# Second pass over an adjacency matrix: units of 8 rows with 2 KB runs in place of 16 rows with 1 KB runs

## The reference, cut to what matters

```
x = layernorm(x + (1 - 0.1 * x - 0.01 * sum(x * (adj @ x), axis=1)))        # layer 0, needs all of adj
x = layernorm(x + gnn(x, adj))                                              # layer 1, needs all of adj again
# in gnn, with A = adj without its diagonal:
node_support = concat(A_pos @ h, A_neg @ h)      # A_pos = (A > 0), A_neg = (A < 0), as 0/1
edge_output  = gru(node_support, h)
att          = softmax over each row of leaky_relu(... a) where A is not zero
edge_support = (att * A) @ (h @ W)
node_output  = gru(edge_support, h)
out          = diag(adj) * edge_output + diag(adj) * node_output
```

## Time and profile before

| | before |
|---|---|
| median of 3 runs | 1680.99 us |
| the profiled execution | 1673.49 us, span 1671.7 us |
| mean granted TensorE clock in it | 0.963 |
| TensorE busy | 1445.0 us (86%) |
| VectorE busy | 1368.0 us (82%) |
| ScalarE busy | 1163.8 us (70%) |
| moved by DMA | 550.18 MB, 329 GB/s over the span |

### The profile page before, as it was taken

One profiled execution on the slowest core, in us unless ns is written; L12 is line 12 of the kernel. 1 busy time (PEld: TensorE's weight loads), 2 busy tenths in 40 slices (PEclk: granted clock), 3 DMA queues, 4 the chain that ended last, 5 costly groups with the idle time before them and its releaser, 6 DMA issues.

```text
span 1671.7 us, 22680 instructions
## 1 busy us (share of the span) xinstructions
PE 1445.0 (86%) x6262; PEld 794.9 (48%) x6262; DVE 1368.0 (82%) x1335; ACT 1163.8 (70%) x1409; POOL 178.0 (11%) x226
## 2 busy tenths in 40 slices
PE   7987878887888888558998899899999899999995
PEld 6655656555555555224444444444444444444442
DVE  5999899898989898647878877887788788778874
ACT  6987979797979797436666666666566666666662
POOL 2000000000001010201101111110111011111100
PEclk9999999999999999779999999999999999999996
DMA  9999999999999999999999999999999999999980
GB/s 264 418 421 422 410 422 409 421 410 421 411 421 413 419 413 419 233 200 333 303 288 306 292 293 296 308 288 291 299 305 298 299 302 295 297 300 310 293 215 11
DMA packets 366090, 550.18 MB, mean 329 GB/s; under 512 B 71024, under 2 KB 333184, under 8 KB 333296
## 3 DMA queue, kind: packets, MB, share of 16 engines
q1 hardware_dynamic: 190672, 408.49, 70.5%
q10 hardware_dynamic: 174976, 141.05, 33.1%
q0 software_dynamic: 416, 0.36, 0.1%
HBM read 545.66 MB, written 4.19 MB: 329 GB/s over the span
## 4 chain that ended last, share of the span: by engine, by line
DMA 30%; issue 21%; ACTq 15%; DVE 15%; PE 9%; ACT 7%; SPq 2%; DVEq 1%; POOL 0%; POOLq 0%
DMA ring<-in_adj 18%; ACTq L247 12%; DMA h_rows<-final 11%; DVE at L806 7%; DVE ps L610 5%; ACT mask L932 5%; PE ps L572 5%; SPq L247 2%; PE ps L1033 2%; ACTq L950 1%; PE ps L539 1%; ACTq L946 1%; PE ps L1045 1%; ACTq L989 0%; ACT final L970 0%
## 5 line engine op out<-in xcount | busy, mean ns | idle before, releaser
L932 ACT ACTIVATE mask<-at 128x2048 fp32r<-128x2048 uint32 x256 | 489.4, 1913 | 281.2 <-DVE at L806 189.6
L572 PE MATMUL ps<-mask,parts 128*128 128x512 f32 x2048 | 552.0, 413 | 101.9 <-DVE ps L610 68.2
L610 DVE SCALAR_TENSOR_TENSOR ps<-ring,ps 128x2048 f32<-128x2048 f32 x256 | 584.3, 2301 | 55.3 <-PE ps L572 34.8
L806 DVE STREAM_TRANSPOSE at<-ring 128x2048 f32<-128x2048 f32 x256 | 577.8, 2290 | 43.6 <-POOL ring L719 37.9
L1033 PE MATMUL ps<-at,hk 128*64 128x512 f32 x2048 | 495.6, 620 | 79.7 <-DVE final L813 42.3
L506 ACT ACTIVATE at<-ring 128x2048 bf16<-128x2048 f32 x256 | 488.7, 1909 | 97.0 <-DMA ring<-in_adj 52.5
L572 PEld LDWEIGHTS ps<-mask,parts 128*128 128x128 f32 x2048 | 374.9, 193 | 278.8 <-DVE ps L610 203.8
L1033 PEld LDWEIGHTS ps<-at,hk 128*64 128x64 f32 x2048 | 148.7, 141 | 346.1 <-issue 250.8
L1045 PE MATMUL ps<-mask,parts 128*128 128x512 f32 x1024 | 270.2, 405 | 13.6 <-ACT final L959 12.9
L1045 PEld LDWEIGHTS ps<-mask,parts 128*128 128x128 f32 x1024 | 182.1, 188 | 152.1 <-issue 73.4
L719 POOL TENSOR_TENSOR ring<-ring,not_diag 128x256 f32<-128x256 f32 x128 | 93.8, 733 | 715.0 <-DMA ring<-in_adj 715.0
(11 more groups left out here) (152 smaller groups left out, 645.4 us busy)
## 6 DMA issues: line engine op xcount, KB each, us to landing
ring<-in_adj SPq DMA_DIRECT2D x256, 1024.0 KB, 16.2
ring<-in_adj SPq DMA_DIRECT2D x264, 512.0 KB, 10.7
ring<-in_adj ACTq DMA_DIRECT2D x248, 512.0 KB, 14.3
stage<-h_rows ACTq DMA_DIRECT2D x16, 128.0 KB, 16.3
nat<-h_rows ACTq DMA_DIRECT2D x16, 128.0 KB, 15.8
out<-final ACTq DMA_DIRECT2D x16, 128.0 KB, 15.4
h_rows<-final ACTq DMA_DIRECT2D x7, 256.0 KB, 22.7
hk<-h_rows ACTq DMA_DIRECT2D x7, 256.0 KB, 23.9
```

What stands on the lines that cost most here:

```text
L572: last = nc.tensor.matmul(ps[:, 4 * (n % 2) + i, :], pair[:, t % 2, e, :], x2[:, cols], start=e == 0, stop=e == 1)
L610: nc.vector.scalar_tensor_tensor(out=gram, in0=ring[:, i % RING, :], scalar=1.0, in1=gram, op0=ALU.mult, op1=ALU.mult, accum_out=flat[:, b ...
L806: nc.vector.transpose(b["at"][:, half % 4, :, :].rearrange("p c (f q) -> p f c q", q=Q), raw[:, :, HC * part:HC * part + HC, :]).then_inc( ...
L932: nc.scalar.activation(b["mask"][:, half % MS, :, :].rearrange("p c i -> p (c i)"), b["at"][:, half % 4, :, :].rearrange("p c i -> p (c i) ...
```

## The change

A unit is now 16 chunks of half the rows of a block: 8 rows for each partition, with runs of 512 columns, 2 KB. It is 2 MB as before, a block still has 8 units, and the ring holds four. Units 2w and 2w + 1 are the two halves of the rows of the same 16 chunks. A transposition takes 8 chunks and 8 rows, still 128 x 2048 elements, and fills one row half of a pair of places of `at`. So TensorE's matmuls, which take 512 rows of one chunk, wait for both transpositions of a pair, and both sign operations. The order of reading is: pair 0 from units 0 and 1, pair 1 from units 0 and 1, and so on; unit 2w comes free after 4w + 3 transpositions, unit 2w + 1 after 4w + 4. The places of `at` and `mask` come free by pairs. The number of instructions and of transfers, and the size of each, stay; a transfer of 512 KB consists of 256 runs instead of 512.

```diff
@@ build_gnn
-    UC = 8
-    U = C // UC
+    UC = 16
     SLOTS = 4
-    HC = UC // 2
+    HC = 4
+    RH = BANK // Q // 2
+    U = 2 * (C // UC)
@@ load_unit
-    RB, UC, GQ, slot = b["RB"], b["UC"], b["GQ"], u % b["SLOTS"]
-    raw = unit_view(b, slot).rearrange("p (f m) -> p f m", f=RB)
+    RH, UC, GQ, slot = b["RH"], b["UC"], b["GQ"], v % b["SLOTS"]
+    wide, rows = v // 2, v % 2
+    raw = unit_view(b, slot).rearrange("p (f m) -> p f m", f=RH)
     for g in groups:
         eng.dma_start(
             raw[Q * g:Q * g + Q, :, :],
-            b["adj"][bass.ds(k * BANK, BANK), GQ * g + UC * Q * u:GQ * g + UC * Q * (u + 1)].rearrange(
+            b["adj"][bass.ds(k * BANK + rows * (RH * Q), RH * Q),
+                     GQ * g + UC * Q * wide:GQ * g + UC * Q * (wide + 1)].rearrange(
                 "(f ii) m -> ii f m", ii=Q)).then_inc(b["s_raw"][prefix][slot], 16)
+def freed(v):
+    return 4 * (v // 2) + v % 2 - 5
+def pair_view(t, pair):
+    at = 2 * (pair % 2)
+    return t[:, at:at + 2, :, :].rearrange("p s c i -> p (s c) i")
@@ First.last_variance
         self.count_signs(dve, grp)
+        dve.wait_ge(self.s["signs_counted"], b["GROUPS"])
@@ Fast.sync
-                sp.wait_ge(s["turned"], k * (2 * U) + 2 * (u + 1 - slots))
+                sp.wait_ge(s["turned"], k * (2 * U) + freed(u))
                 load_unit(sp, b, "f_", k, u, (0, 1))
@@ Fast.vector, turn
-            u, part = half // 2, half % 2
-            if part == 0:
-                dve.wait_ge(s["diagonal_out"], k * self.U + u + 1)
+            pair, rows = half // 2, half % 2
+            v = 2 * (pair // 2) + rows
+            if pair % 2 == 0:
+                dve.wait_ge(s["diagonal_out"], k * self.U + v + 1)
             if not (first and half < 4):
-                dve.wait_ge(s["weighed_done"], n - 3)
-                dve.wait_ge(s["mask_ready"], n - 3)
-            raw = unit_view(b, u % b["SLOTS"]).rearrange("p (f c q) -> p f c q", f=RB, q=Q)
+                dve.wait_ge(s["weighed_done"], n - rows - 2)
+                dve.wait_ge(s["mask_ready"], n - rows - 2)
+            raw = unit_view(b, v % b["SLOTS"]).rearrange("p (f c q) -> p f c q", f=RH, q=Q)
+            to = pair_view(b["at"], pair)[:, :, RH * Q * rows:RH * Q * (rows + 1)]
             nc.vector.transpose(
-                b["at"][:, half % 4, :, :].rearrange("p c (f q) -> p f c q", q=Q),
-                raw[:, :, HC * part:HC * part + HC, :]).then_inc(s["turned"], 1)
+                to.rearrange("p c (f q) -> p f c q", q=Q),
+                raw[:, :, 2 * HC * (pair % 2):2 * HC * (pair % 2 + 1), :]).then_inc(s["turned"], 1)
@@ Fast.scalar, sign
-                act.wait_ge(s["added_done"], n - MS + 1)
+                act.wait_ge(s["added_done"], n - half % 2 - 2)
+            cols = slice(RH * Q * (half % 2), RH * Q * (half % 2 + 1))
             nc.scalar.activation(
-                b["mask"][:, half % MS, :, :].rearrange("p c i -> p (c i)"),
-                b["at"][:, half % 4, :, :].rearrange("p c i -> p (c i)").bitcast(U32), ACT.Sign,
-                accum_out=b["seen"][:, bass.ds(n, 1)]).then_inc(s["mask_ready"], 1)
-            u = half // 2 + SLOTS
-            if half % 2 == 1 and (u < U or not last):
+                pair_view(b["mask"], half // 2)[:, :, cols], pair_view(b["at"], half // 2)[:, :, cols].bitcast(U32),
+                ACT.Sign, accum_out=b["seen"][:, bass.ds(n, 1)]).then_inc(s["mask_ready"], 1)
+            u = 2 * (half // 4 + 2) + half % 2
+            if half % 4 >= 2 and (u < U or not last):
                 load_unit(act, b, "f_", k + u // U, u % U, (2, 3))
@@ Fast.tensor, weigh and add
-            pe.wait_ge(s["turned"], k * H + half + 1)
+            pe.wait_ge(s["turned"], k * H + half - half % 2 + 2)
...
-            pe.wait_ge(s["mask_ready"], k * H + half + 1)
+            pe.wait_ge(s["mask_ready"], k * H + half - half % 2 + 2)
```

More of the change, by code:

```diff
@@ L239, in _, with load_unit @@
                 full.vector(dve)
-def load_unit(eng, b, prefix, k, u, groups=(0, 1, 2, 3)):
-    RB, UC, GQ, slot = b["RB"], b["UC"], b["GQ"], u % b["SLOTS"]
-    raw = unit_view(b, slot).rearrange("p (f m) -> p f m", f=RB)
+def load_unit(eng, b, prefix, k, v, groups=(0, 1, 2, 3)):
+    RH, UC, GQ, slot = b["RH"], b["UC"], b["GQ"], v % b["SLOTS"]
+    wide, rows = v // 2, v % 2
+    raw = unit_view(b, slot).rearrange("p (f m) -> p f m", f=RH)
     for g in groups:
@@ L712, in no_diagonal @@
 def no_diagonal(nc, pool, b, prefix, k, u):
-    U, UC, SLOTS = b["U"], b["UC"], b["SLOTS"]
-    raw = unit_view(b, u % SLOTS)[:, (u % 2) * UC * (UC * Q):(u % 2 + 1) * UC * (UC * Q)]
-    diag = bass.AP(tensor=raw.tensor, offset=raw.offset, ap=[list(raw.ap[0]), [UC * Q + Q, UC], [1, Q]])
+    U, UC, RH, SLOTS = b["U"], b["UC"], b["RH"], b["SLOTS"]
+    start = (u % 2) * RH * Q
+    raw = unit_view(b, u % SLOTS)[:, start:start + Q]
+    diag = bass.AP(tensor=raw.tensor, offset=raw.offset, ap=[list(raw.ap[0]), [UC * Q + Q, RH], [1, Q]])
     pool.wait_ge(b["s_raw"][prefix][u % SLOTS], (k * (U // SLOTS) + u // SLOTS + 1) * (16 * G))
@@ L720, in no_diagonal @@
         out=diag, in0=diag,
-        in1=b["not_diag"][:, bass.ds(k + (U // 2 - 1 - u // 2), 1), :].to_broadcast([P, UC, Q]), op=ALU.mult)
+        in1=b["not_diag"][:, bass.ds(k + (U // 2 - 1 - u // 2), 1), :].to_broadcast([P, RH, Q]), op=ALU.mult)
 ACC_T, ACC_S, ACC_C = 0, 1, 2
@@ L752, in sync @@
                 rows_back(sp, b, last)
-            sp.wait_ge(s["turned"], 2 * (u + 1 - slots))
+            sp.wait_ge(s["turned"], freed(u))
             load_unit(sp, b, "f_", 0, u, (0, 1))
@@ L785, in vector @@
         nc, b, s, ps = self.nc, self.b, self.s, self.b["ps"]
-        H, HC, RB = self.H, b["HC"], b["RB"]
+        H, HC, RH = self.H, b["HC"], b["RH"]
         lo, hi = slice(0, D), slice(D, P)
@@ L917, in scalar @@
         nc, b, s, ps = self.nc, self.b, self.s, self.b["ps"]
-        H, U, MS, SLOTS = self.H, self.U, b["MS"], b["SLOTS"]
+        H, U, MS, RH = self.H, self.U, b["MS"], b["RH"]
         lo, hi = slice(0, D), slice(D, P)
@@ L1146, in sync @@
             if u >= slots:
-                sp.wait_ge(s["turned"], 2 * (u + 1 - slots))
+                sp.wait_ge(s["turned"], 4 * (u // 2 - 1))
             load_unit(sp, b, "g_", 0, u)
@@ L1150, in sync @@
             for u in range(U):
-                sp.wait_ge(s["turned"], k * (2 * U) + 2 * (u + 1 - slots))
+                sp.wait_ge(s["turned"], k * (2 * U) + 4 * (u // 2 - 1))
                 load_unit(sp, b, "g_", k, u)
@@ L1173, in turn @@
             n = k * H + half
-            u, part = half // 2, half % 2
+            wide, part = half // 4, half % 4
             if part == 0:
-                dve.wait_ge(s["diagonal_out"], k * self.U + u + 1)
-            raw = unit_view(b, u % b["SLOTS"]).rearrange("p (f c q) -> p f c q", f=RB, q=Q)
+                dve.wait_ge(s["diagonal_out"], k * self.U + 2 * wide + 2)
+            raw = b["ring"][:, 4 * (wide % 2):4 * (wide % 2) + 4, :].rearrange("p r m -> p (r m)").rearrange(
+                "p (f c q) -> p f c q", f=RB, q=Q)
             nc.vector.transpose(
```

## The result

The changed kernel takes 1710.0 us (median of four runs, 1704.6 to 1715.5) against 1681.4 us. The ratio is 1.0177, with a 95% interval from 1.0134 to 1.0221. The forecast was 1640 us and "faster": wrong in sign, and outside the range of 1615 to 1700. The profiled execution took 1704.56 us.

What follows compares the result with a forecast made beforehand. TensorE and DMA were taken as near their limits, with ScalarE stalled by its full queue. From 1673.5 us, 41 for the blocks and 2 for the seam came off, giving 1630.5; plus 7.5, 1638, said as 1640; range 1615 to 1700.

Steps and rivals of the forecast that it cites:

- The limit and the waits: Second pass: TensorE and DMA near a limit; ScalarE stalls on its full queue, so `reset` waits 6.0 us a block.
- Runs of 2 KB: Unit loads with both queues busy: rate rises from 348 to 385 GB/s, fast part of a block from 37.6 to 34.0 us.
- The slow part I leave alone.: DMA with one queue idle or moving small rows: 19.8 us a block at 206 GB/s, taken as unchanged.
- I charge 0.6 us a block for late units.: Ring of units: lead falls from 6 transpositions to 5, 21.5 to 17.9 us; late units cost 0.6 us a block.
- Stalls of ScalarE: ScalarE's load issues: room counted in runs, so four fifths of the 6.0 us ahead of `reset` goes, 4.8 us a block.
- The pair rule: TensorE's weigh waits for both transpositions: 3.1 us a block if VectorE stays, vanishing with `reset` 4.8 us earlier.
- Rival C: Weigh of pairs 5 and 7: pair waits bind, up to 3.1 us a block, 1727 us or half, 1704; chance 0.17.
- The signs: Trace checks: right by issues below 600 ns, 380 GB/s slices, short line 853 waits; wrong by 348 plateau, weigh idle, late units.
- TensorE's own need: One block of the second pass on TensorE without waiting: 53.4 us, so at most 4.0 us a block to gain.
- The seam: Between the passes, 670 to 760 us: between 8 us less and 8 more, taken as 2 less.
- The sum: Second pass block: 54.1 + 0.6 = 54.7 us, 2.7 less, 41 us over 15 blocks.
- Rival B: Loads: length gives little, 348 GB/s being queues meeting, so VectorE waits for units; 1665 to 1695 us, middle 1681; chance 0.15.

Runs made afterwards that it cites:

- a: Kernel before with only the loads in 2 KB runs, old order and waits; fastest run 1708.2 us with the clock falling, 56.4 us a block in the first seven.
- e: Changed kernel with the three small transfers of each block (nat, stage, out) cut to 16 runs, first stage load whole; 1607.6 us.
- k: a with the three small transfers of each block cut as in f; 1600.3 us.
- c: a plus the new reading order of units and their freeing, without the pair rule; 1725.1 us, ratio to the kernel before 1.0214.
- g: Changed kernel with the three small transfers whole but in runs of 1 KB instead of 256 bytes; 1632.0 us.
- d: a plus the pair rule alone, old reading order; fastest run 1701.6 us with the clock falling, 57.3 us a block in the first seven.
- f: Kernel before with the three small transfers of each block cut to 16 runs, first stage load whole; 1599.9 us, ratio 0.9577.
- h: Kernel before with the three small transfers whole but in runs of 1 KB instead of 256 bytes; 1600.2 us.
- j: h with the result made right by strided matmuls and a second copy of the diagonal; 1618.9 us, ratio 0.9664 to the kernel before.
- i: Kernel before with the small row loads nat and stage issued on POOL's queue instead of ScalarE's; 1640.5 us, ratio 0.9808.

## Why the prediction was wrong, point by point

- **The limit and the waits** were read rightly: ScalarE's full queue was what held up the kernel. What it was full of I didn't ask. The page's last part lists three small transfers a block on that queue, each landing after some 16 us, and the rate row showed where they passed; I named them ("idle or moves small rows") and went on. The one for the kernel before:

```profile
nat<-h_rows ACTq DMA_DIRECT2D x16, 128.0 KB, 15.8
```

- **Runs of 2 KB**: 385 GB/s forecast for both queues; the plateau is 351 to 382, 369 on average. Nearly right.
- **"The slow part I leave alone."** This step failed. I held the 19.8 us at 206 GB/s of a block fixed while I changed the runs of the other queue. They take turns with the small runs, so the small phase grew, by the estimate above from 7.9 to 14.8 us a block, and catching up by one queue alone came behind it (in the stretch shown, 4 us at 212 GB/s). The fast part gained 3.6 us by my sum, 2.1 at the measured 369 GB/s. The slow part took more than that back in the changed kernel, though not in a.
- **"I charge 0.6 us a block for late units."** This step failed with it. VectorE waits 149.2 us for units, 9.9 a block, and only 6.0 of that stand where the wait of `reset` was. The fall of the lead from 6 transpositions to 5 was seen; what it costs depends on the small transfers ahead of the units. Without them the whole new order costs 0.8 us a block (e against k), with them and runs of 2 KB 4.6 (c against a, first seven blocks).
- **Stalls of ScalarE**: four fifths were to go. The median issue did fall from 1580 to 348 ns, but the longest is 8281 ns, and the wait of the signs for issues rose, 84.5 to 99.8 us. Where the small transfers are gone or in longer runs, the stalls nearly vanish: the longest issue of a unit load on ScalarE's queue is 567 ns in e, 625 in g and 2323 in k. My ground for counting room in runs was also read too well: one of SyncE's megabyte issues in the first pass took 7.1 us.
- **The pair rule** was priced at 0.7 us a block above the TensorE limit, with the `at` places. d has 0.9 more than a in the first seven blocks (its third block, 60.6 us, stands at a granted clock of 0.92), the changed kernel no more than c. The size was right. Rival C, which made the pair rule the cause of a loss, has 1704 us among its times, near the measured 1710; that is luck, since its mechanism isn't the one that the runs show.
- **The signs** misled. Of the signs of being right, the issue below 600 ns, the wait of line 853 (now 0.2 us in all) and a plateau with slices of 380 came true, and the time still rose. Of the signs of being wrong, two came true: VectorE waits for units by 9.9 us a block, and TensorE waits at weigh for VectorE, 3.7 us a block. The second was put down to rival C, but c is as long without the pair rule, so that wait isn't what made the time.
- **TensorE's own need**, 53.4 us a block, was 52.5 (f, h, k).
- **The seam**: the first `weighed_sum` came 1.6 us earlier (775.6 against 777.2); 2 forecast.
- **The sum**: a gain of 2.7 us a block became a loss of 2.1.
- Rival B's middle, 1681, fails for the reason that the plateau did rise. What was missing is a rival with the queues' turns in it.

## What to carry to other kernels

Ask of each DMA queue what it carries, in runs and not in bytes. Here two queues took turns run by run, and a small run cost 82 ns beside runs of 1 KB and 154 beside runs of 2 KB, with everything behind it in its own queue waiting. Longer runs for the bulk make that worse, and whether it is felt depends on how soon the next unit is needed: in the old order the longer runs were a gain all the same. So first lengthen the small runs, or give them a queue that carries nothing urgent; here that was worth 3.4% (j) and 1.9% (i), where the change itself cost 1.8%. And look whether a trace is of one piece before you take a mean over it: the mean of a over all blocks, 59.6 us, is that of two parts with different clocks, and says the opposite of its first part.

## What the runs showed of the hardware that I had not expected

- Turns of one run for one run between two queues, at 256 bytes against 2 KB as at 256 bytes against 1 KB (625 to 626, 388 to 389).
- One queue that writes 32 partitions at a time makes 206 to 212 GB/s with runs of 1 KB and of 2 KB alike; two, on different halves of the partitions, 348 and 369.
- Small transfers of 1% of the bytes took 4% of the time (f, ratio 0.9577).
- Runs of 2 KB alone made a block shorter (56.4 us for 58.0), the new reading order alone changed nothing (57.9), and both together made it longer (61.0), all in the first seven blocks.
